# Three PE waits and the vector engine's unit wait on instructions of their own, and the last base tile by Pool's queue

## What is computed

```
xn = layernorm(x)
q, k, v = heads(xn @ Wq.T + bq), heads(xn @ Wk.T + bk), heads(xn @ Wv.T + bv)
attn = softmax(q * 16**-0.5 @ k.T) @ v  -> @ Wo.T + bo
ffn  = sum_e weight_e(xn) * ((silu(xn @ Wg_e) * (xn @ Wu_e)) @ Wd_e)
out  = x + attn + ffn
```

## Time and profile before

| | us |
|---|---|
| median of 3 runs | 6732.64 |
| lowest and highest | 6714.23 and 6736.91 |
| the profiled execution | 6725.33 |
| its span in the trace | 6723.5 |
| token phase ends, attention begins | about 1402 |
| attention loop (first and last pair of `st` matmuls) | 1499 to 6619 |
| output phase | 6644 to 6723 |

### The profile page before, as it was taken

One profiled execution on the slowest core, in us unless ns is written; L12 is line 12 of the kernel. 1 busy time (PEld: TensorE's weight loads), 2 busy tenths in 40 slices (PEclk: granted clock), 3 DMA queues, 4 the chain that ended last, 5 costly groups with the idle time before them and its releaser, 6 DMA issues. The chain is left out here.

```text
span 6723.5 us, 138330 instructions
## 1 busy us (share of the span) xinstructions
PE 6529.0 (97%) x57168; PEld 3116.2 (46%) x57168; DVE 5737.6 (85%) x6099; ACT 4989.0 (74%) x9109; POOL 517.3 (8%) x542
## 2 busy tenths in 40 slices
PE   7999999969999999999999999999999999999996
PEld 6888888833333333333333333333333333333334
DVE  5544545469999999999999999999999999999972
ACT  3333333318888888888888888888888888888884
POOL 2222222200000000000000000000000000000000
PEclk9999999969999999999999999999999999999998
DMA  2111111111111111111111111111111111111104
GB/s 93 45 45 45 45 45 45 38 28 27 32 32 33 33 30 29 29 29 29 29 29 29 29 29 29 29 29 29 33 32 32 33 34 33 29 29 29 29 10 156
DMA packets 239852, 246.98 MB, mean 37 GB/s; under 512 B 154537, under 2 KB 199849, under 8 KB 232873
## 3 DMA queue, kind: packets, MB, share of 16 engines
q1 hardware_dynamic: 227184, 203.41, 13.6%
q0 software_dynamic: 12032, 34.61, 2.1%
HBM read 159.26 MB, written 76.58 MB: 35 GB/s over the span
## 5 line engine op out<-in xcount | busy, mean ns | idle before, releaser
L888 DVE TENSOR_REDUCE mx<-sc 128x1 f32<-128x1024 f32 x4096 | 5003.1, 1224 | 131.4 <-PE sc L775 84.5
L871 ACT ACTIVATE pr<-st 128x512 f32<-128x512 f32 x8192 | 4448.2, 595 | 638.0 <-PE st L784 447.5
L797 PE MATMUL pv<-pr,vst 128*32 128x256 f32 x32768 | 2621.5, 392 | 12.4 <-ACT oT L858 11.8
L784 PE MATMUL st<-experts 50*128 50x512 f32 x8192 | 2045.2, 496 | 24.2 <-ACT pr L871 14.6
L775 PE MATMUL sc<-experts 48*128 48x512 f32 x8192 | 1656.2, 400 | 52.0 <-DVE mx L888 27.1
L784 PEld LDWEIGHTS st<-experts 50*128 50x128 f32 x8192 | 767.3, 183 | 1731.4 <-ACT pr L871 1677.0
L797 PEld LDWEIGHTS pv<-pr,vst 128*32 128x32 f32 x32768 | 644.9, 108 | 1499.1 <-issue 765.2
L775 PEld LDWEIGHTS sc<-experts 48*128 48x128 f32 x8192 | 792.9, 189 | 92.3 <-DVE mx L888 64.4
L432 ACT ACTIVATE gated<-gate 128x512 f32<-128x512 f32 x256 | 152.0, 598 | 633.3 <-PE up L76 633.1
L600 DVE TENSOR_TENSOR hraw<-gated,up 128x512 f32<-128x512 f32 x256 | 173.2, 686 | 431.6 <-ACT gated L432 429.0
L76 PE MATMUL gate<-xT,experts 128*128 128x512 f32 x1536 | 408.4, 402 | 11.2 <-issue 11.2
(11 more groups left out here) (99 smaller groups left out, 1292.4 us busy)
## 6 DMA issues: line engine op xcount, KB each, us to landing
experts<-parts_d SPq DMA_DIRECT2D x372, 256.0 KB, 4.2
parts_d<-part SPq DMA_DIRECT2D x64, 512.0 KB, 3.0
x_in<-in_L_attn_hidden_states SPq DMA_DIRECT2D x16, 512.0 KB, 4.6
v_d<-v_sb SPq DMA_DIRECT2D x32, 256.0 KB, 2.2
base_d<-base SPq DMA_DIRECT2D x16, 512.0 KB, 3.6
vst<-v_d SPq DMA_DIRECT2D x128, 64.0 KB, 2.2
sums_d<-oT SPq DMA_DIRECT2D x256, 32.0 KB
whole<-sums_d POOLq DMA_DIRECT2D x32, 256.0 KB, 3.0
```

The source lines that it names most:

```text
L784: nc.tensor.matmul(st[(x + grp) % STB][:, :], kr[par][r0:r0 + ROWSM, kb * P:(kb + 1) * P], qr[par][r0:r0 + ROWSM, q0:q0 + GT], start=True, ...
L797: last = nc.tensor.matmul(pv[VC * j:VC * (j + 1), cols], vst[par][:, kb, :], pr[:, (QSUB * kb + j) % PRING, cols], start=(kb == 0 and half ...
L871: nc.scalar.activation(pr[:, (QSUB * kb + j) % PRING, :], st[x % STB][:, :], ACT.Exp).then_inc(st_read, 1)
L888: nc.vector.reduce_max(mx[par][:, u // MAXU, u % MAXU:u % MAXU + 1], sc[g % 2][:, :], AX.X).then_inc(sc_read, 1)
```

## The change

Four waits go from `wait_ge` to `wait_alone`: the three of PE in `score_pair`, `max_unit` and `times_v`, and that of the vector engine's `max_unit`. Apart from that the end of the token phase is rearranged. The last base tile is stored by Pool's queue right behind the last `down_used`, with a semaphore of its own. SP issues only parts 0 and 1 of the first head's rows there; parts 2 and 3 and the ones move to the start of SP's list in the attention phase, ahead of its loads of v.

```diff
@@ SP, token phase
                 if last:
+                    for i in range(2):
+                        sp.wait_ge(parts_stored[i], (SPLITS // 2 * NG + 1) * DMA)
                     sp.wait_ge(gu_full, NG * E * KC)
-                    first_head(sp)
-                wait_alone(sp, down_used, (g + 1) * E * 2 + 2, passed)
-                sp.dma_start(tokens_of(c.base_d, g), base[par][:, :, :]).then_inc(base_stored[par], DMA)
+                    first_head(nc, c, (0, 1))
+                else:
+                    wait_alone(sp, down_used, (g + 1) * E * 2 + 2, passed)
+                    sp.dma_start(tokens_of(c.base_d, g), base[par][:, :, :]).then_inc(base_stored[par], DMA)
             rolled(sp, before, body)
+            sp.wait_ge(last_base_stored, DMA)
@@ Pool, token phase
             rolled(pool, before, body)
+            pool.wait_ge(down_used, NG * E * 2 + 2)
+            pool.dma_start(tokens_of(c.base_d, NG - 1), base[1][:, :, :]).then_inc(last_base_stored, DMA)
@@ SP, attention phase
             sp.sem_inc(sums_stored, DMA)
+            first_head(nc, c, (2, 3))
+            for par in range(RING):
+                for grp in range(2):
+                    r0 = 64 * grp + TERMS
+                    sp.dma_start(kr[par][r0:r0 + 2, :].bitcast(F32), c.ones_d).then_inc(c.ones_in, DMA)
             sp.wait_ge(v_cols, 4)
@@ PE, attention phase
-                pe.wait_ge(sc_read, g - 1 + SC_PRE)
+                wait_alone(pe, sc_read, g - 1 + SC_PRE, passed_sc)
...
-                pe.wait_ge(st_read, s * SLOTS + x + 1 - STB + 2 + READ_PRE)
+                wait_alone(pe, st_read, s * SLOTS + x + 1 - STB + 2 + READ_PRE, passed_st)
...
                 if half == 0:
-                    pe.wait_ge(st_read, s * SLOTS + slot_of(kb, QSUB - 1, final) + 2 + READ_PRE)
+                    wait_alone(pe, st_read, s * SLOTS + slot_of(kb, QSUB - 1, final) + 2 + READ_PRE, passed_pv)
@@ DVE, attention phase
-                dve.wait_ge(sc_full, g + 1)
+                wait_alone(dve, sc_full, g + 1, passed_units)
```

More of the change, by code:

```diff
@@ L89, in head_rows, with first_head @@
                              c.parts_d[w, ORDER[w][term], n * HD:(n + 1) * HD, c0:c0 + cols])
+def first_head(nc, c, parts):
+    for part_n in parts:
+        w, half = ((0, 0), (1, 0), (1, 1), (0, 1))[part_n]
+        for grp in range(2):
+            for term in range(3):
+                head_rows(nc, c, w, 0, 0, grp, term, half * QH, QH).then_inc(c.first_in[part_n], DMA)
 def setup_phase(nc, a, c):
@@ L250, in token_phase @@
         base_stored = [sem(f"base_stored{i}") for i in range(2)]
+        last_base_stored = sem("last_base_stored")
         vchain = sem("vector_chain")
@@ L279, in store_parts @@
                                  part[u % 2][:, :, :].bitcast(F32)).then_inc(parts_stored[u % 2], DMA)
[L281 to L292, removed]
             def store_v(g):
@@ L318, in body @@
                 if last:
+                    for i in range(2):
+                        sp.wait_ge(parts_stored[i], (SPLITS // 2 * NG + 1) * DMA)
                     sp.wait_ge(gu_full, NG * E * KC)
-                    first_head(sp)
-                wait_alone(sp, down_used, (g + 1) * E * 2 + 2, passed)
-                sp.dma_start(tokens_of(c.base_d, g), base[par][:, :, :]).then_inc(base_stored[par], DMA)
+                    first_head(nc, c, (0, 1))
+                else:
+                    wait_alone(sp, down_used, (g + 1) * E * 2 + 2, passed)
+                    sp.dma_start(tokens_of(c.base_d, g), base[par][:, :, :]).then_inc(base_stored[par], DMA)
             rolled(sp, before, body)
+            sp.wait_ge(last_base_stored, DMA)
             for i in range(2):
-                sp.wait_ge(base_stored[i], (NG // 2 + 1) * DMA)
+                sp.wait_ge(base_stored[i], (NG // 2 + 1 - i) * DMA)
                 sp.wait_ge(parts_stored[i], (SPLITS // 2 * NG + 1) * DMA)
@@ L653, in attention_phase @@
         passed = sem("passed_a")
+        passed_units = sem("passed_units")
+        passed_st, passed_sc, passed_pv = (sem(f"passed_{n}") for n in ("st", "sc", "pv"))
         QK_LOADS = 2 * 3 * 2
```

## The result

The changed kernel takes 6941.26 us (median of 4 runs, 6934.16 to 6946.9), beside 6734.77 for the kernel before on the same chip. The ratio is 1.0296, with a 95% interval of 1.028 to 1.0311: 207 us slower. The forecast was 6918 in a range of 6832 to 6990.

A forecast was written before the change was run, and what follows sets the result against it. The PE and ACT ring was taken to bound half 0, PE's own order half 1. Loop +201 us, last 40 key blocks +3, waits already alone -5, boundary -14: net +185 on 6732.6, 6918 us, range 6832 to 6990.

The forecast's parts named there:

- Half 0, +0.06: Loop, first half step: `score_pair`'s wait alone lengthens the PE and ACT ring by 0.06 us, 1.24 to 1.30.
- Half 1, +0.04: Loop, second half step: 1.23 to 1.27 us, from `score_pair`'s wait (1.25 at least) and `max_unit`'s wait.
- I take 0.02: Cost in us of `max_unit`'s wait alone between `st` and `sc`, counted in half 1 only; bounds 0 and 0.05.
- the high end: Nothing of `max_unit`'s wait overlaps: +0.13 us per key block, +245 us; sign: `sc` load 0.15 or more behind `st`.
- `times_v` and `max_unit` at nothing: PE's loop waits, satisfied early: `times_v` alone costs nothing; `max_unit` costs nothing attached, 0.02 us alone in half 1.
- DVE: Reduction's wait alone: starts perhaps 0.06 us later, costs nothing in the loop; sign: idle before L888 up some 0.04 a unit.
- it just fits: Units ahead of the loop: PE's and DVE's waits add 0.12 us together, within the 0.15 left, so no cost.
- The 2 us named as the price of a miss: Ahead of the loop, if the added waits didn't fit: 80 units with 0.03 us each, 2 us.
- The boundary: End of the token phase: rearranged store and loads let attention begin about 1387, 14 us less (bounds 12 and 18).
- half the price: Rival: waits behind `st` and the second load's 0.03 are swallowed, only half 0 pays; 6837 us, chance 0.15.
- Nothing changes: Rival: loop unchanged (compiler restores the wait or sequencer is quicker), only the boundary counts; 6719 us, chance 0.07.
- Faster: Rival: `st` weight loads slide under the `pv` passes, 94 us less, if exponential to load is under 0.07; 6638 us, chance 0.08.

The follow-up runs named there:

- The dose of two waits: Kernel before the change, with `score_pair`'s wait put alone on PE's sequencer and written twice in a row: 7526.99 us beside 6740.07, 1.1161.
- the same with the shift: Kernel before with `score_pair`'s wait alone, plus five counting-only PE instructions once in each half head, to shift instruction transfers: 6982.12 us beside 6740.07, 1.0362.

## Why the prediction was right, and where it wasn't

**Half 0, +0.06:** right. 1.309 was measured for 1.30, from the 0.11 between exponential and load of the earlier trace rows, measured as 0.114. The dose of two waits confirms the mechanism.

**Half 1, +0.04:** right in size (1.266 for 1.27), wrong in its parts. The step "I take 0.02" for `max_unit`'s wait failed: it measures zero in a typical step. What the earlier trace rows gave for half 1 with the one wait, 1.25, was 0.02 too low. That row is of the first key block, and its `pv` came 0.68 behind `st`; in the typical half 1 it is 0.70. So PE's order, not the exponential, bounds half 1, and the `st` load there is 0.133 behind the exponential, not the 0.11 that I had named for both halves. The sign that I had named for the high end, an `sc` load 0.15 behind that of `st`, did come and meant nothing, because the `sc` matmuls start 0.31 behind those of `st` with it or without.

**`times_v` and `max_unit` at nothing, as far as cover goes:** this is the step that failed most. Attached or alone, the wait is satisfied, and I asked only who waits for it then. I didn't ask what the sequencer's lead was good for. With the `st` wait left on its load, these two cost 106 us. In the changed kernel the bill is smaller than the parts: +259 for one, +106 for two, but +225 in the loop for all. By the medians the typical steps make 197 of it (0.064 and 0.034, or 0.049 for each of 4016), where the sum had +199. For the other 28 the sum had no term. What long steps have above typical ones went from 45 us to 80. This missing term is about the size of the difference between 6918 and 6941. Why the pauses over 0.45 us inside a group are 23 without the `st` wait, 12 with it alone and 1 with all, isn't settled.

**DVE:** right in the loop: alone its wait costs nothing. The sign that I had named, more idle time before a reduction, came (from 131 us to 322 on the page, 0.048 for each of 4016 units, expected 0.04) but proves nothing of this wait: with `score_pair`'s wait alone it is 326, because the steps are longer. What DVE's wait does is shift the reduction, from 0.043 behind `sc`'s end to 0.149 in the loop. That is 0.11, not the 0.06 that I took from ACT. So ahead of the loop "it just fits" failed: the units came each 1.16 us instead of 1.13, and 80 units took 2.4 us more. It takes both waits: with DVE's alone it is 0.6 us, with PE's alone 0.1. The 2 us named as the price of a miss were right.

**The boundary:** right. 14 were forecast and 16.4 seen in this trace; alone it is 15.6 us in device time. The store landed in 6.4 us, within the 3.3 to 8.3 of the earlier trace rows, and the 16 moved issues cost nothing.

**The rivals:** "half the price" is out, since half 1 grew too. "Nothing changes" is out by 9577 waits. "Faster" would have decided at 0.07 between exponential and load; it measured 0.114. The rule of the Trainium skill behind it (TensorE: Matmul & The Clock Gate, Architectural detail), that weight loads are pulled ahead, changed nothing here: `pv` to `st` stayed at 0.57 to 0.61 (3208.97 to 3209.54, 3207.66 to 3208.27). The high end, which I had drawn from the Trainium skill's lifecycle rule (Perfetto Trace Analysis, Per-instruction lifecycle), didn't come for `max_unit`'s wait: its 51 ns did push the `sc` load by 0.04, as the rule has it, but not the `sc` matmuls. At the `st` wait written twice nothing overlapped.

## What to carry to other kernels

A wait that is satisfied last belongs on the instruction that needs it: alone on the sequencer it put 0.06 us on each round of a ring of two engines. A wait that is always satisfied isn't sure to be free alone either: two of them on PE, which bounds this kernel, cost 106 us, one on DVE, which doesn't, nothing. What fits is that on its own it holds the sequencer back, and the engine's queue no longer covers whatever delays the sequencer; five counting instructions cost 10 us with that cover and some 200 without. Make the two halves of a change into two kernels: here the rearranged boundary with attached waits (0.9977) beats both.

## What the runs showed of the hardware that I had not expected

- An instruction that only counts up a semaphore is recorded at 51 ns on PE, but they follow each other 0.151 us apart: 0.755 for five. The second of two stand-alone waits costs 0.15 as well. The recorded length isn't the price.
- PE's instructions come in packets of 16 KB, one for 256 instructions, every 13.3 us before the change (301 in 4000) and 12.6 after it (318). With PE waits alone on the sequencer PE stood idle for up to 2.4 us (without the `st` wait), 3.65 us (with it alone) and 3.4 us (the same with the shift), each time until 1.4 to 1.7 us behind such a packet. Two kernels with such waits have no pause of this kind.
- The clock can fall with such a pause: granted 0.50 for 41 us after 1.6 us of standstill, and for 164 us with one of 2.6 us near the end of the loop (PE busy for 14.25 of the 17 us before). It can fall there without one too: for 106 us in the changed kernel with five counting instructions (PE busy for 21.66 of 27 us before) and for 92 us with the twice written wait, both without idle time of PE above 0.6 us ahead of the fall. In 40 us at 0.50 PE did 228 matmuls, in the next 40 us at 1.00 385.
